# A transformer block with a rotated attention and a mixture of experts: V's rotation moved from matrix products to elementwise work on row tiles

## The reference, cut to what matters

```python
sa, ca, ga, sb, cb, gb = the six rows of (silu(c) @ wmod) of the batch   # 256 features each
h = layernorm(x) * (1 + ca) + sa
def givens_rotate(r, x):          # r: 256 numbers, one (c, s) for each pair of features
    y0 = c * x[0::2] - s * x[1::2]
    y1 = c * x[1::2] + s * x[0::2]
q, k, v = givens_rotate(rot_w[0], h), givens_rotate(rot_w[1], h), givens_rotate(rot_w[2], h)
attn = softmax((2 + 2 * q @ k.T) / scale + bias)
ave = attn @ v
x = x + ga * ave / |ave|
h2 = layernorm(x) * (1 + cb) + sb
x = x + gb * (16 experts on chosen rows of h2, plus a shared gated layer on all rows)
```

## Time and profile before

| | |
|---|---|
| median of three runs | 2467.9 us |
| span of the profiled execution | 2465.3 us |
| phase A in it | about 0 to 1300 us |
| TensorE busy (matmuls) | 96% |
| VectorE, ScalarE, GpSimd busy | 64%, 42%, 47% |
| one batch in phase A, first to last transposes | 38.1 us for most |
| TensorE clock granted, mean | 0.987 of full |

### The profile page before, as it was taken

How to read it: one execution, slowest core, us unless ns; L and a number is a source line. 1 busy time by engine, 2 the same in 40 slices (tenths; PEclk the granted TensorE clock), 3 DMA queues, 4 the chain that set the end, 5 groups by cost and what they waited for, 6 DMA issues and landing times.

```text
span 2465.3 us, 40995 instructions
## 1 busy us (share of the span) xinstructions
PE 2372.3 (96%) x14388; PEld 2086.3 (85%) x14388; DVE 1567.9 (64%) x3198; ACT 1032.8 (42%) x1912; POOL 1150.4 (47%) x997
## 2 busy tenths in 40 slices
PE   6999999999998999999987999999999999999997
PEld 5888888888887888888876888888888888888886
DVE  6677767778776877788846455555554545555553
ACT  3545545444553545545442333333333333333332
POOL 1233333333332333333352666666666666666664
PEclk9999999999998999999998999999999999999999
DMA  2111111111111111111115444443444444434433
GB/s 90 53 44 59 51 60 60 52 51 57 54 61 44 60 43 60 52 60 60 59 62 90 86 90 82 88 84 66 79 84 87 86 85 88 84 60 86 84 62 43
DMA packets 78506, 167.03 MB, mean 68 GB/s; under 512 B 11744, under 2 KB 46720, under 8 KB 78368
## 3 DMA queue, kind: packets, MB, share of 16 engines
q0 software_dynamic: 49152, 67.14, 16.7%
q1 hardware_dynamic: 29216, 97.85, 11.8%
HBM read 97.71 MB, written 67.24 MB: 67 GB/s over the span
## 4 chain that ended last, share of the span: by engine, by line
PE 84%; DVE 6%; issue 4%; POOL 2%; DMA 1%; ACT 1%; SPq 0%; DVEq 0%; POOLq 0%; ACTq 0%
PE ps L349 26%; PE ps L351 26%; PE ps L350 26%; PE ps L501 2%; DVE stage L856 2%; PE ps L387 1%; DVE bn_stats L758 1%; PE ps L420 1%; DMA stage<-in_wd 1%; DVE x_t L753 1%; PE ps L442 1%; DVE hidden L753 1%; POOL rstd L1144 1%; POOL out L1209 1%; ACT x_t L693 0%
## 5 line engine op out<-in xcount | busy, mean ns | idle before, releaser
L349 PE MATMUL ps<-x_t,weights 128*128 128x512 f32 x1536 | 617.3, 402 | 23.2 <-DVE hidden_f L1111 13.3
L350 PE MATMUL ps<-x_t,weights 128*128 128x512 f32 x1536 | 602.5, 392 | 0.0
L351 PE MATMUL ps<-x_t,weights 128*128 128x512 f32 x1536 | 601.8, 392 | 0.0
L1209 POOL DMA_INDIRECT out<-x_rows,step_token x256 | 418.1, 1633 | 333.9 <-DVE x_rows L1090 275.4
L349 PE MATMUL ps<-weights,hidden 128*128 128x256 f32 x1536 | 435.8, 284 | 8.7 <-POOL hidden L1148 5.6
L351 PE MATMUL ps<-weights,hidden 128*128 128x256 f32 x1536 | 436.1, 284 | 0.0
L350 PE MATMUL ps<-weights,hidden 128*128 128x256 f32 x1536 | 436.0, 284 | 0.0
L1111 DVE TENSOR_TENSOR hidden_f<-gelu,ps 128x512 f32<-128x512 f32 x256 | 175.7, 686 | 379.0 <-ACT gelu L733 348.1
L733 ACT ACTIVATE gelu<-ps 128x512 f32<-128x512 f32 x256 | 152.8, 597 | 535.8 <-PE ps L351 508.4
L349 PEld LDWEIGHTS ps<-x_t,weights 128*128 128x128 f32 x1536 | 290.6, 189 | 83.6 <-DVE hidden_f L1111 13.5
L1148 POOL TENSOR_TENSOR hidden<-hidden_f,hidden 128x512 fp32r<-128x512 f32 x128 | 165.5, 1293 | 408.7 <-ACT hidden L647 408.7
(11 more groups left out here) (174 smaller groups left out, 4436.9 us busy)
## 6 DMA issues: line engine op xcount, KB each, us to landing
x_rows<-in_x SPq DMA_DIRECT2D x32, 512.0 KB, 3.5
pairs<-mod_rows SPq DMA_DIRECT2D x32, 512.0 KB, 4.3
h_rows<-stage SPq DMA_DIRECT2D x32, 512.0 KB, 2.6
out<-y_rows SPq DMA_DIRECT2D x32, 512.0 KB, 2.9
stage<-in_wg SPq DMA_DIRECT2D x16, 512.0 KB, 3.4
stage<-in_wd SPq DMA_DIRECT2D x16, 512.0 KB, 4.4
stage<-in_wu SPq DMA_DIRECT2D x16, 512.0 KB
x_rows<-h_rows,step_token POOLq DMA_INDIRECT x256
```

Of the source, the lines that this page charges most:

```text
L349: pe.matmul(o, lhs(HI), rhs(HI), start=start, stop=False)
L350: pe.matmul(o, lhs(HI), rhs(LO), start=False, stop=False)
L351: return pe.matmul(o, lhs(LO), rhs(HI), start=False, stop=stop)
L1209: pool.indirect_dma_start(out=out_rows, out_offset=bass.IndirectOffsetOnAxis(ap=ICUR[g][:, t:t + 1], axis=0), in_=X1[:, g % 2, t * D:(t + ...
```

## The change

- V is no longer made by TensorE. `ln1_rows` (VectorE) writes the modulated rows `h` themselves, with eight instructions: four for `(x - mean) * (1 + ca)` and four for `* rstd + sa`. Both take the batch's `ca` and `sa` as rows on all partitions (`MOD1`), which SyncE loads for each batch (256 KB) after the norm before has been written.
- TensorE transposes those rows directly, and the transposed form needs no modulation: ScalarE copies it rounded (`h1_high`), VectorE subtracts (`h1_low`), each for a half k, both from PSUM. K is made and split by halves too.
- GpSimd rotates the rows: `h * s` into `V_SWAP`, `h * c` into `V_ROWS`, and the sum of the second with the first, its pairs of features exchanged, back into `V_ROWS`. Each is one instruction on 128x1024. The first two stand in `iteration(i-1)` around `hidden_lo(.., 1)`, the sum in `iteration(i)` after the second norm's 1/sqrt.
- HI of V is made by ScalarE from SBUF after the four exponentials, LO of V by VectorE after the second norm. `scores` no longer waits for V, the first half of attention times V does.
- K and V lie in `W[1]`, `ROTV` goes, and the setup makes the first batch's `ca`, `sa` rows by two products with the condition spread over 128 columns, the rotation's rows by four small ones, and two more products for `sa` and `ca` of all batches.

The diff, cut to its core:

```diff
@@ sync: iteration @@
+                if valid(i + 1) and not (isinstance(i, int) and i < 1):
+                    wait(sp, h1r_ready, i + 1)
+                    sp.dma_start(MOD1[:, :, :].rearrange("p m d -> p (m d)"),
+                                 mod_dram[bass.ds(i + 1, 1), 0:2 * D].to_broadcast((P, 2 * D))).then_inc(mod1_in, 16)
@@ tensor @@
-            def k_and_v(n):
+            def keys(n):
                 if at(n, 0):
                     pe.wait_ge(rot_ready, 1)
-                wait(pe, h1_hi, n + 1)
-                wait(pe, h1_lo, n + 1)
                 for k in range(KD):
+                    wait(pe, h1_hi, n * KD + k + 1)
+                    wait(pe, h1_lo, n * KD + k + 1)
                     mm = mm3(PC[:, (KD + k) * S:(KD + k + 1) * S], lambda a: ROTK[:, a, k, :],
                              lambda a: H1_T[:, a, k, :], True, True)
-                mm.then_inc(k_done, 1)
-                for t in range(T):
-                    for k in range(KD):
-                        mm = mm3(PC[:, t * D + k * P:t * D + (k + 1) * P],
-                                 lambda a: H1_T[:, a, k, t * P:(t + 1) * P], lambda a: ROTV[:, a, k, :], True, True)
-                mm.then_inc(v_done, 1)
+                    mm.then_inc(k_done, 1)
 
             def scores(n):
...
-                wait(pe, v_hi, n + 1)
-                wait(pe, v_lo, n + 1)
@@ scalar: iteration @@
                         act.activation(EXPS[:, t, :], PC[:, t * S:(t + 1) * S], ACT.Exp, bias=NB[:, t:t + 1],
                                        accum_out=Z[:, t:t + 1]).then_inc(exp_done, 1)
+                    v_high(i)
@@ vector @@
-            def ln1_apply(n, p):
+            def ln1_rows(n, p):
...
+                dve.wait_ge(mv1, n + 1)
+                wait(dve, mod1_in, n * 16)
+                wait(dve, xt_done, n * KD)
+                wait(dve, h1r_read, n)
+                for t in range(T):
+                    last = dve.scalar_tensor_tensor(H1R[:, t, :], X[:, p, t * D:(t + 1) * D], MV[0][:, t, 0:1],
+                                                    MOD1[:, CA, :], ALU.subtract, ALU.mult)
+                last.then_inc(cent1, 1)
+                dve.wait_ge(cent1, n + 1)
                 dve.wait_ge(rs1, n + 1)
-                wait(dve, xt_done, n)
                 for t in range(T):
-                    last = dve.tensor_scalar(XN[:, t, :], X[:, p, t * D:(t + 1) * D], MV[0][:, t, 0:1],
-                                             RS[0][:, t:t + 1], ALU.subtract, ALU.mult)
-                last.then_inc(xn_ready, 1)
+                    last = dve.scalar_tensor_tensor(H1R[:, t, :], H1R[:, t, :], RS[0][:, t:t + 1],
+                                                    MOD1[:, SA, :], ALU.mult, ALU.add)
+                last.then_inc(h1r_ready, 1)
@@ vector: iteration @@
                 if valid(i - 1):
                     ln2_apply(i - 1, 1 - p)
+                if valid(i):
+                    v_low(i)
                 if valid(i - 2):
                     wait(dve, y_stored, (i - 2) * 16)
@@ gpsimd @@
+            def v_swap_part(n):
...
+                pool.tensor_tensor(V_SWAP, H1R, ROT_ROWS[:, 1, :].unsqueeze(1).to_broadcast((P, T, D)),
+                                   ALU.mult).then_inc(v_parts, 1)
+            def v_own_part(n):
...
+                pool.tensor_tensor(V_ROWS[:, :, :], H1R, ROT_ROWS[:, 0, :].unsqueeze(1).to_broadcast((P, T, D)),
+                                   ALU.mult).then_inc(h1r_read, 1)
+            def v_sum(n):
...
+                pool.tensor_tensor(rows, rows, V_SWAP.rearrange(pairs_of, j=2)[:, :, :, ::-1],
+                                   ALU.add).then_inc(v_rotated, 1)
@@ gpsimd: iteration @@
                     rstd(1, mv2, ve2, rs2, i - 1)
+                if valid(i):
+                    v_sum(i)
...
                     hidden_lo(i - 1, 0)
+                if valid(i + 1):
+                    v_swap_part(i + 1)
+                if valid(i - 1):
                     hidden_lo(i - 1, 1)
+                if valid(i + 1):
+                    v_own_part(i + 1)
```

More of the change, by code:

```diff
@@ L37 @@
 WCOLS = KD * F
-NMOD = 4
-GA, SB, CB, GB = range(NMOD)
+NMOD = 6
+SA, CA, GA, SB, CB, GB = range(NMOD)
 EPS = 1e-5
@@ L364, in _, with rotation_rows @@
             pe.wait_ge(wmod_in, 16)
-            for j in range(2):
-                for m in range(KD):
-                    n = j * KD + m
+            for k in range(KD):
+                mm = pe.matmul(PC[:, 0:2 * D], CACT_T[:, k, 0:1].to_broadcast((P, P)), WMOD[:, k, 0:2 * D],
+                               start=k == 0, stop=k == KD - 1)
+            mm.then_inc(saca_ps, 1)
+            def rotation_rows():
+                pe.wait_ge(rot_cols, 1)
+                for j, cols in ((0, COS[:, 2, :]), (1, CS[:, 3, :])):
                     for k in range(KD):
-                        mm = pe.matmul(PG[:, n * B:(n + 1) * B], WMOD[:, k, j * D + m * P:j * D + (m + 1) * P],
-                                       CACT_T[:, k, :], start=k == 0, stop=k == KD - 1)
-            mm.then_inc(saca_ps, 1)
+                        mm = pe.matmul(PG[:, j * D + k * P:j * D + (k + 1) * P], cols[:, k:k + 1].to_broadcast((P, P)),
+                                       IDENT, start=True, stop=True)
+                mm.then_inc(rot_rows_ps, 1)
             def modulations():
@@ L378, in modulations @@
                                        WMOD[:, k, 2 * D + n * 512:2 * D + (n + 1) * 512], start=k == 0, stop=k == KD - 1)
+                for k in range(KD):
+                    mm = pe.matmul(PG[0:B, 512:1024], CACT_T[:, k, :], WMOD[:, k, 0:2 * D],
+                                   start=k == 0, stop=k == KD - 1)
                 mm.then_inc(mods_ps, 1)
             def x_transposes(n):
-                wait(pe, xn_ready, n + 1)
+                wait(pe, h1r_ready, n + 1)
                 wait(pe, at_hi, n * T)
@@ L426, in a_times_v @@
                     pe.wait_ge(mods_raw, 1)
+                if half == 0:
+                    wait(pe, v_hi, n + 1)
+                    wait(pe, v_lo, n + 1)
                 for t in (2 * half, 2 * half + 1):
@@ L786, in _ @@
             dve.wait_ge(saca_ps, 1)
[L787 to L789 removed]
+            dve.tensor_copy(MOD1[:, SA, :], PC[:, 0:D])
+            dve.tensor_scalar(MOD1[:, CA, :], PC[:, D:2 * D], 1.0, None, ALU.add).then_inc(mod1_first, 1)
             def rotations():
@@ L828, in modulations @@
                 dve.wait_ge(mods_raw, 1)
-                cb = mods[:, CB * D:(CB + 1) * D]
-                dve.tensor_scalar(cb, cb, 1.0, None, ALU.add)
+                for j in (CA, CB):
+                    one = mods[:, j * D:(j + 1) * D]
+                    dve.tensor_scalar(one, one, 1.0, None, ALU.add)
                 for j in (GA, GB):
@@ L1056, in iteration @@
                     odd = 0 if len(rounds) == 2 else 1 - p
+                    wait_apart(dve, top_kept, before)
                     top_best(odd)
@@ L1065, in iteration @@
                 if len(rounds) > 1:
+                    wait_apart(dve, top_kept, rounds[1][2])
                     top_best(1)
```

150 lines of the change are left out of this document (84 added, 66 removed).

## The result

The kernel after takes 2545.8 us (median of four runs, 2539.1 to 2551.6), the kernel before in the same runs 2469.7: ratio 1.031, 95% interval 1.029 to 1.033. The profiled executions span 2539.5 and 2465.3 us. It is slower, by the mechanism of the forecast (a), and some 31 us less slow than it said, inside the range that (a) gave itself (2535 to 2610).

What follows compares the result with a forecast made beforehand. TensorE was taken as the bound by a hair, VectorE's chain closing at the same place. Batch terms plus clock loss gave 42.1 us periods: (42.1 - 38.15) x 28 - 2 = +109 us, forecast 2577, range 2450 to 2610.

Steps and rivals of the forecast that it cites:

- (a): GpSimd gets in at both places, second norm and first norm: 2577 us, own range 2535 to 2610, chance 0.47.
- The two meetings: GpSimd stops VectorE: sum of V at the second norm, 2.3 us; addition to Y at the first norm, loss 2.05.
- (b): GpSimd gets in at the first norm only, VectorE keeping its four second-norm instructions together: 2512 us, chance 0.22.
- Rival (c): VectorE's overlapping instructions keep GpSimd out of a norm, or exclusion doesn't hold for their form: 2420 us, chance 0.18.
- The plain period: Walk around one batch before clock loss: 38.4 us, or 40.7 with the sum of V in the way.
- LO of V: Between the second norm and L1028; LO of the transposes starts 3.55 us after the norm, not 2.8: loss 0.75.
- The first norm: Eight VectorE instructions, 3.35 us, plus 0.2 of waits and 2.4 for GpSimd's addition to Y: loss 2.05.
- The clock: After idle time before the transposes, some seven TensorE products run at half clock: 1.4 us lost each time, bounds 0 and 3.
- The top rounds: In 16 batches the top round comes before the split, and up to 1.0 us sticks out.
- The setup: First norm 2.1 us longer, two more products, batches 0 and 1 spared V's waits and products: net -2 us, -6 to +4.
- Rival (e): Exchanged pairs make the sum of V twice as long: 2.4 us more in 28 batches, 2644 us, chance 0.05.
- The bound by a hair: TensorE, busy 96%, barely bounds the kernel before; VectorE's chain closes at the same place, the transposes, after 0.27 us idle.

Runs made afterwards that it cites:

- both edits: Kernel after, with GpSimd's addition to Y ahead of the first norm's 1/sqrt and the sum of V waiting for the second norm's first half: 2428.2 us (0.984).
- the kernel with the shorter plain period (38.6 us): Kernel after, with only the sum of V made to wait for the second norm's first half: 2520.3 us (ratio 1.021).

## Why the prediction was right, and where its sizes were off

**The two meetings** are the term that decides. The prediction took +2.3 for the sum of V and, net, +2.05 for the first norm with the addition to Y. Taking away the second gave 2.18 a batch; the first shows as 2.2 us in L930's group and in the kernel with the rotation cut. That the sum would get in at a seam of a group that VectorE had begun was the open point between (a) and (b); it does, after the first of four. Rival (c) is excluded by the same rows. (Of the 32 L877 that the prediction drew on, 20 and not 22 are longer than 0.3 us; all 20 end 0.02 us behind an L1148.) The Trainium skill (SBUF — State Buffer, Who interferes with whom) lets whoever issues first have the shared pair for a whole instruction. The rows agree, if that is read of one instruction and not of a group. TensorE's idle time is near what was said: 2.48 us at the transposes for 3, and 0.43 + 1.14 at the second transposes and before the gate for 1.6.

**The plain period** was to be 40.7 before the clock, and is 40.03. Two terms make up the difference. LO of V: LO of the transposes starts 3.21 us behind L940's end (396.76 to 399.97), not 3.55; I had summed durations where starts follow each other closer than that (397.63, 398.78, 399.97), and HI of V came 0.13 sooner: 0.34 together. The first norm takes 5.63 us from its start to the transposes, two groups of 1.67 and 2.2 of standing, and was reckoned at 5.97, with 2.4 of standing and 0.2 of waits that didn't come: 0.34. The walk was also made around a batch of 37.91 us and its end compared with 38.15, which made the forecast's step some 0.2 us too small.

**The clock** was right in size and wrong in frequency. I took 1.4 us in every batch; it costs 1.2 to 1.6 without a top round, but it fell in 13 of the 27 periods (a granted clock of 0.95 to 0.97, 1.00 in the others), while I had counted the loss in all 27. The eight transposes take 1.87 us or more in 9 of the 28 periods and 1.06 to 1.10 in all the others but one, after the same 2.48 us of idle time (410.96 and 452.15 above). Why one batch falls and the next doesn't, no run here settles.

**The top rounds** were named in the working, "up to 1.0 us sticks out", and then left out of the forecast's sum. They cost 1.0 us, and in 12 of them the attention output waited for the factor. There are 19 periods with a top round, not the 16 that the working took. That this term and the clock's came out near each other is luck, the two errors offset: over the plain period the 27 come out 1.34 us longer in the mean, of which 0.19 stood there before, so 1.15 where I had 1.4.

**The sum** then is +3.11 us a period (1.96 plain, 1.15 besides) against +3.95, which is 84.0 instead of 107 us over 27 periods, and most of the miss.

**The ends.** The setup was to give 2 us and took 3.6: batch 0's transposes came 2.5 us later (the first norm, as reckoned), batch 1's period gave only 1.65, and batches 2 and 3 took 2.8 more, since the meetings begin there; I had them start with batch 3. I called phase B unchanged, and 9.0 us went behind the last transposes. V's products of batch 31 stood there, 2.6 us, and early in phase B one wait of TensorE shrank by 11 us, before and after:

```profile
1329.35 0.79 PE L349 MATMUL ps<-x_t,weights 128*128 128x512 f32 x1 [13.32 <-DVE hidden_f L1111]
```
```profile
1405.24 0.50 PE L363 MATMUL ps<-x_t,weights 128*128 128x512 f32 x1 [2.26 <-DVE hidden_f L1149]
```

In both, the chain that ended last goes through a transfer of expert weights ahead of it (stage<-in_wd, 23.30 us long before, 16.83 after). The wait is 10.28 us in the kernel before with the addition ahead, and 2.31 us with the change and both edits, so it goes with the change; why, no run here shows. Smaller pieces go the other way. The loop's end gained 4.4 us, within the 10 that I had left for it.

**Rival (e)**, exchanged pairs at twice the time, is excluded: the sum takes 2.40 us, as the plain addition does.

**"The bound by a hair"** holds, and the runs put a number to it: of 2.3 us of products 1.1 are won, with the old meeting at the first norm or without it. I had priced that old meeting as a part of the period to be kept; removing it alone, with every product left in, wins 25 us, and the prediction didn't look at that.

## What to carry to other kernels

Before work goes to GpSimd, lay its instructions over VectorE's at the minute where they will run, and look on the critical chain for steps with two SBUF inputs, and for copies and tensor_scalars from SBUF to SBUF, tiny ones too; a 2.4 us instruction cost up to 2.2 us wherever it met such a step, whoever was first, and nothing beside steps that read PSUM. Then ask what TensorE's idle time behind it does to the clock, which here cost some 1.5 us each time it fell. Look also whether such a meeting is there already: here the cheapest gain was one existing instruction moved by a place in a queue. A removed matmul is worth only what the next wait behind it leaves, so put that wait's size beside it.

## What the runs showed that I had not expected

- Two SBUF inputs aren't needed: the kernel before's L856 is a tensor_scalar with one tile of rows and two numbers per partition, and its first instruction took 2.48 us beside L1183 instead of 0.40. The norm's statistics, with one SBUF input too, kept their 0.41 us beside L1186 (L779 at 387.40, L1186 from 387.27 to 388.57 in the kernel after).
- VectorE's smallest steps are shut out too: the bias on 128x2 went from 0.29 to 1.34 us, the copy of 128x16 took 1.28 us in a top round and L1006 on 128x16 2.43 instead of 0.22, each until GpSimd's instruction ended.
- The two take turns instruction by instruction: GpSimd got in after VectorE's first of four, having waited 0.25 us, and VectorE's next stood for each of two GpSimd instructions in a row.
- GpSimd's 1/sqrt on four columns did not hold VectorE: L883's first instruction started at 405.33 beside L1182 (404.71 to 405.75), took its usual 0.48 us, and the group lost no more than the 2.2 us of the addition to Y. L952 kept its 0.29 us at 389.58 beside the other 1/sqrt (388.84 to 389.90).
- The same 2.48 us of idle time brought TensorE down to 1.2 GHz in some batches and not in others, and the kernel with the shorter plain period (38.6 us) lost the clock more often than the one with 40.03: in 20 of 27 periods against 13. With the rotation cut, 2.3 to 2.7 us of idle time at the same place in every batch cost the clock in 6 of 27. With both of GpSimd's products in a row, 2.25 to 2.5 us before quarter 1 went with a lower clock in every top round but the first.
